# Setup divided into stages, constant products placed in TensorE's gaps, and all five queues reordered, in a four-layer graph network on one core

## What is computed

```
x = layernorm(x + L0(x, adj))     # multi-head attention, 4 heads of 32, scores masked by adj
x = layernorm(x + L1(x, adj))     # graph attention: e = leaky_relu(s1[i] + s2[j]), masked softmax, @ h
x = layernorm(x + L2(x, adj))     # the same with 8 heads of 16, a log prior, output projection W_out
x = layernorm(x + L3(x, adj))     # relu(x@w1+b1); unmasked attention (256 wide) + elu + residual;
                                  # relu(@w2+b2); masked attention (128 wide) + elu + residual; relu
```

## Time and profile before

| | |
|---|---|
| median of 3 runs | 1126.12 us (1124.22 to 1127.83) |
| profiled execution, its own time | 1126.89 us |
| its span, first to last instruction | 1125.1 us |
| TensorE busy | 997.7 us (89%) |
| VectorE busy | 917.5 us (82%) |
| ScalarE busy | 734.3 us (65%) |
| GpSimd busy | 397.1 us (35%) |
| mean granted TensorE clock | 0.970 |

### The profile page before, as it was taken

One profiled execution on the slowest core, in us unless ns is written; L12 is line 12 of the kernel. 1 busy time (PEld: TensorE's weight loads), 2 busy tenths in 40 slices (PEclk: granted clock), 3 DMA queues, 4 the chain that ended last, 5 costly groups with the idle time before them and its releaser, 6 DMA issues.

```text
span 1125.1 us, 26002 instructions
## 1 busy us (share of the span) xinstructions
PE 997.7 (89%) x8821; PEld 727.6 (65%) x8821; DVE 917.5 (82%) x2530; ACT 734.3 (65%) x1901; POOL 397.1 (35%) x781
## 2 busy tenths in 40 slices
PE   2899888999999999999999999999999998778673
PEld 1566655858677776767676776767676867455452
DVE  4467979988899898989889998989898988876432
ACT  1698756766768686877768685867777674432522
POOL 0113233323443342625243433426252334341421
PEclk9999989999999999999999999999999999988976
DMA  4001111102020202011020202020020202010000
GB/s 121 1 11 59 39 58 29 68 20 68 29 67 11 82 15 77 20 46 52 20 72 25 67 12 76 20 72 26 31 66 11 71 17 67 20 66 20 10 0 19
DMA packets 30994, 46.77 MB, mean 42 GB/s; under 512 B 7824, under 2 KB 10128, under 8 KB 30736
## 3 DMA queue, kind: packets, MB, share of 16 engines
q1 hardware_dynamic: 30864, 45.11, 12.8%
HBM read 40.64 MB, written 4.46 MB: 40 GB/s over the span
## 4 chain that ended last, share of the span: by engine, by line
PE 34%; DVE 25%; issue 8%; POOL 4%; ACT 3%; DVEq 0%; ACTq 0%; POOLq 0%
DVE P L1147 15%; PE bank L633 8%; PE bank L592 7%; PE bank L491 4%; PE bank L538 2%; POOL e L1308 2%; DVE stats_l L1006 2%; PE bank L470 2%; PE bank L499 2%; DVE l_P L1058 1%; ACT x L769 1%; PE bank L462 1%; DVE v L1178 1%; POOL rstd_l L1274 1%; DVE h_t L1183 1%
## 5 line engine op out<-in xcount | busy, mean ns | idle before, releaser
L1147 DVE SCALAR_TENSOR_TENSOR P<-row,t2e,mask_t 128x512 f32<-128x512 f32 x512 | 358.6, 760 | 18.3 <-DMA row<-line 15.3
L724 ACT ACTIVATE probs<-probs,neg_max 128x512 f32<-128x512 f32 x256 | 183.6, 718 | 13.1 <-DVE neg_max L970 13.0
L962 DVE CUSTOM_DVE_ANT_0 probs<-bank,mask_add 128x512 f32<-128x512 f32 x256 | 168.9, 676 | 13.0 <-PE bank L491 12.9
L734 ACT ACTIVATE probs_t<-bank 128x512 f32<-128x512 f32 x256 | 149.2, 601 | 10.8 <-PE bank L499 10.8
L499 PE MATMUL bank<-ident,probs 128*128 128x128 f32 x1024 | 137.4, 275 | 13.9 <-ACT probs L724 12.6
L769 ACT ACTIVATE x<-x,shift_l,rstd_l 128x128 f32<-128x128 f32 x256 | 105.3, 483 | 62.9 <-POOL shift_l L1281 62.8
L1308 POOL TENSOR_SCALAR e<-v 128x128 f32<-128x128 f32 x128 | 77.4, 632 | 171.2 <-ACT v L816 171.2
L499 PEld LDWEIGHTS bank<-ident,probs 128*128 128x128 f32 x1024 | 114.1, 141 | 28.9 <-ACT probs L724 24.5
L1266 POOL TENSOR_TENSOR rstd_l<-mv_l,ln_eps 128x4 f32<-128x4 f32 x64 | 19.3, 302 | 298.2 <-DVE mv_l L1016 298.1
L592 PE MATMUL bank<-P,GH 128*32 128x512 f32 x1024 | 117.4, 599 | 5.5 <-DVE P L1147 2.8
L633 PE MATMUL bank<-t,l_P 128*128 128x257 f32 x512 | 119.1, 383 | 1.1 <-DVE l_P L1072 1.1
(11 more groups left out here) (161 smaller groups left out, 1901.8 us busy)
## 6 DMA issues: line engine op xcount, KB each, us to landing
row<-line SPq DMA_DIRECT2D x128, 256.0 KB, 3.7
x_in<-in_x SPq DMA_DIRECT2D x16, 256.0 KB, 2.8
out<-x SPq DMA_DIRECT2D x16, 256.0 KB, 2.0
l_P<-in_adj SPq DMA_DIRECT2D x1, 1024.0 KB, 4.8
line<-turned SPq DMA_DIRECT2D x64, 4.0 KB, 1.5
w_fc<-in_L_gnn_W_fc SPq DMA_DIRECT2D x1, 256.0 KB, 3.4
probs_t<-in_L_gnn_a_fc SPq DMA_DIRECT2D x1, 256.0 KB, 6.1
w_cat<-in_L_gnn_W SPq DMA_DIRECT2D x2, 64.0 KB, 3.4
```

Source lines behind the costliest of these rows:

```text
L724: act.activation(e, e, ACT.Exp, bias=neg_max[:, m:m + 1], scale=SCALE0, accum_out=g.of(den0)[:, m:m + 1])\
L734: act.activation(probs_t[c % 2][:, h, :, :].rearrange("p j n -> p (j n)"), ps("l0_t", g, m)[:, :], ACT.Copy)\
L962: dve.tensor_tensor_reduce(probs[c % 2][:, h, :], ps("l0_s", g, m)[:, :], mask_add[:, c, :], 1.0, -3.0e38, ALU.add, ALU.max, row_max[:, m: ...
L1147: last = dve.scalar_tensor_tensor(P2[:, h % GROUP2, j, :], row(g, h)[:, :], g.of(t2e)[:, j, h:h + 1], mask_t[:, j, :], ALU.max, ALU.mult)
```

## The change

The setup becomes stages of the queues, with a semaphore each. On SP, nine loads (five weights and the four layer 0 biases) come first, on s_proj; then, as turns of SP's order, adj_load (the adjacency) and late_loads (fifteen loads for layers 1 to 3, on l1_in, l2_in, l3_in); then x. TensorE first makes twelve products of constants (WARM_UP) while it waits, transposes the five weights, waits for ScalarE's copies and starts its turns; the four mask blocks are the turns mask_T. VectorE's masks, folds and prior steps are turns (add_mask, one_mask, fold1, fold2, fold3, prior_in, prior_out). Its order begins: add_mask, one_mask, fold1, l0_v of graph 0, fold2, one l0_max, fold3, one l0_max, prior_in, two l0_max, l0_neg. The first user of each result waits for it, for graph 0 alone. The folds read their vectors from P2 instead of probs_t.

TensorE's order gets 102 turns "warm" (letter Z). Each makes two 128-column products of the identity and ones into the bank of the next stage, behind the wait for that bank and ahead of the stage's own waits; the stage then overwrites it. They stand in the new order as follows: one each before l0_xT(1), l0_k(1) and l0_t(0); two before l0_t(3, 12), behind l2_y(0); and 97 from l0_t(15, 12) on, among them 6 before l3b_o of graph 14, 16 before l3_zT of graph 15, 3 before its l3b_s, 6 before its l3b_o and 13 before its l3_r, the last turn of TensorE.

The order strings of all five engines and the banks are new throughout. The work of the stages themselves is as before. In TensorE's new order, of graph 9 for instance, l0_q follows l0_xT by five transposes of exponentials, where it followed by some forty turns; l2_h and l3_m1 have likewise moved close behind l2_xT and l3_xT.

The diff, cut to its core:

```diff
+WARM_UP = 12
...
     "pe":
-        "a0c0b0d0a1e0e0c1b1d1f0f0f0f0e0f0g0f0f0f0e0f0f0g0f0f0e1f0f0g0f0f0e1f1g0h0f1f1i0f1e1f1f1f1g1f1e1j0a2f1"
...
+        "a0b0c0d00000e0e000Z0a1b1Z0c100d1Z0f0f0f0f0e0f0g0f0f0f0e0f0f0g0f0f0e1f0f0g0f0f0e1g0h0f1f1i0f1f1e1f1f1"
...
+        "Z0Z0Z0Z0Z0Z0DfDfZ0IeEfFfFfGfZ0Z0Z0HfZ0Z0Z0Z0Z0Z0JfJfZ0Z0Z0Z0Z0Z0Z0Z0Z0Z0Z0Z0Z0If",
...
     for name, g, k in turns("pe"):
+        if name == "warm":
+            continue
...
-            sp.dma_start(adj_i, adj.rearrange("(p c) n -> p c n", c=C)).then_inc(s_adj, 16)
...
+            def adj_load(g, k):
+                sp.dma_start(adj_i, adj.rearrange("(p c) n -> p c n", c=C)).then_inc(signal["adj_in"], 16)
+
+            def late_loads(g, k):
+                l1, l2, l3 = signal["l1_in"], signal["l2_in"], signal["l3_in"]
+                sp.dma_start(w1_cat[:, 2:2 + D], w["L1_gnn_W"]).then_inc(l1, 16)
...
             pe.wait_ge(s_const, 3)
-            pe.wait_ge(s_w, 16 * N_WEIGHT_DMAS)
+            for _ in range(WARM_UP):
+                pe.matmul(bank[BANKS - 1][:, 0:P], ident[:, :], ones[:, :], start=True, stop=True)
+            pe.wait_ge(s_proj, 16 * N_PROJECTION_DMAS)
...
-            pe.wait_ge(s_setup, 2)
+            pe.wait_ge(s_proj_t, 1)
+
+            def mask_T(g, j):
+                pe.wait_ge(*sig("one_mask", g, 1))
+                ps = empty("mask_T", g, j)
                 for c in range(C):
-                    last = pe.transpose(bank[0][:, c * P:(c + 1) * P], adj_m[:, c, j * P:(j + 1) * P], ident[:, :])
-                last.then_inc(s_pre_pe, 1)
+                    last = pe.transpose(ps[:, c * P:(c + 1) * P], adj_m[:, c, j * P:(j + 1) * P], ident[:, :])
+                last.then_inc(filled("mask_T", g, j), 1)
...
+            def keep_warm(stage, g, k):
+                ps = empty(stage, g, HEADS0 * k if stage == "l0_s" else k)
+                for c in range(2):
+                    pe.matmul(ps[:, c * P:(c + 1) * P], ident[:, :], ones[:, :], start=True, stop=True)
+
+            order = turns("pe")
+            for at, (name, g, k) in enumerate(order):
+                if name == "warm":
+                    keep_warm(*next(turn for turn in order[at:] if turn[0] != "warm"))
+                else:
+                    stages[name](g, k)
...
+            def fold3(g, k):
+                dve.wait_ge(*sig("l3_in", g, 9 * 16))
+                for q in range(2):
+                    fold_in(w3_fc[:, q, 0:1], w3_fc[:, q, 2:2 + HID], foldv[:, 512:768])
+                    fold_in(w3_fc[:, q, 1:2], w3_fc[:, q, 2:2 + HID], foldv[:, 768:1024])
+                fold_in(w3_hand[:, 0:1], w3_hand[:, 2:2 + D], foldv[:, 1024:1152])
+                fold_in(w3_hand[:, 1:2], w3_hand[:, 2:2 + D], foldv[:, 1152:1280])
+                dve.memset(folds[:, 2:3], 0.0).then_inc(signal["fold3"], 1)
```

More of the change, by code:

```diff
@@ L305, in build_program @@
         stored = [sem(f"stored{q}") for q in range(2)]
-        for name, n in [("x_biased", 1), ("neg_max0", 4), ("exp0", 16), ("den0_safe", 1), ("rden0_made", 1),
+        for name, n in [("adj_in", 16), ("l1_in", 2 * 16), ("l2_in", 4 * 16), ("l3_in", 9 * 16), ("add_mask", 1), ("one_mask", 1),
+                        ("fold1", 1), ("fold2", 1), ("fold3", 1), ("prior_in", 1), ("prior_exp", 1), ("prior_ln", 1),
+                        ("prior_out", 1), ("x_biased", 1), ("neg_max0", 4), ("exp0", 16), ("den0_safe", 1), ("rden0_made", 1),
                         ("l2_c4", 1), ("dmax8_diag", 1), ("small2_made", 2), ("exp2", 3), ("gh2", 1), ("rden2_made", 2), ("p2_made", HEADS2),
@@ L530, in l0_y, with project @@
                 last.then_inc(filled("l0_y", g), 1)
-            def project(stage, src, before, cat, width):
+            def project(stage, src, before, cat, width, folded):
                 def f(g, k):
@@ L612, in l3_m1 @@
                 pe.wait_ge(*took("l3_xT", g))
+                if g.i == 0:
+                    pe.wait_ge(*sig("l3_in", g, 9 * 16))
                 ps = empty("l3_m1", g, k)
@@ L621, in l3_h @@
                     pe.wait_ge(*took("l3_m1", g, 1))
+                if c == 0 and g.i == 0:
+                    pe.wait_ge(*sig("fold3", g, 1))
                 ps = empty("l3_h", g, c)
@@ L673, in _ @@
                 "l3_o": l3_o, "l3_zT": l3_zT, "l3_m2": l3_m2,
-                "l3_h2": project("l3_h2", out2_t, "l3_m2", w3_hand, D + 2), "l3b_dm": spread_max("l3b"),
+                "l3_h2": project("l3_h2", out2_t, "l3_m2", w3_hand, D + 2, "fold3"), "l3b_dm": spread_max("l3b"),
                 "l3b_s": spread_sources("l3b"), "l3_r": l3_r, "l3b_o": attend("l3b", t4),
             }
-            for name, g, k in turns("pe"):
-                stages[name](g, k)
+            def keep_warm(stage, g, k):
[8 more added lines that the diff above has]
+                    stages[name](g, k)
         @block.scalar
@@ L799, in l3_m1 @@
                 act.wait_ge(*wrote("l3_m1", g, k))
+                if g.i == 0:
+                    act.wait_ge(*sig("l3_in", g, 9 * 16))
                 if g.has(1):
@@ L954, in l0_max @@
                 dve.wait_ge(*wrote("l0_s", g, m))
+                if g.i == 0 and m == 0:
+                    dve.wait_ge(*sig("add_mask", g, 1))
                 if c < 2:
@@ L1141, in l2_p @@
                     dve.wait_ge(*sig("exp2", g, 3))
+                    if g.i == 0:
+                        dve.wait_ge(*sig("fold3", g, 1))
                     if g.has(1):
@@ L1214, in _ @@
             stages = {
+                "add_mask": add_mask, "one_mask": one_mask, "fold1": fold1, "fold2": fold2, "fold3": fold3,
+                "prior_in": prior_in, "prior_out": prior_out,
                 "l0_v": l0_v, "l0_max": l0_max, "l0_neg": l0_neg, "l0_den": l0_den, "l0_rcp": l0_rcp, "l0_o": l0_o,
```

378 lines of the change are left out of this document (194 added, 184 removed), and 8 rows, old and new, of the table STAGES.

## The result

| | before | after |
|---|---|---|
| median | 1126.6 us (4 runs, 1124.2 to 1127.8) | 1097.56 us (4 runs, 1097.38 to 1098.13) |
| span of the profiled execution | 1125.1 us | 1095.9 us |
| VectorE busy | 917.5 us | 925.4 us |
| mean granted TensorE clock | 0.970 | 0.985 |

The ratio of after to before is 0.9746, with an interval of 0.9729 to 0.9763: 29.0 us faster than the runs beside it, where 12.5 were forecast.

What follows compares the result with a forecast made beforehand. TensorE was taken to bound the middle, so other edits could win only at the two ends. From 1126.12 us, -3.5 (start) - 9.5 - 1 (clock) - 1 (order) + 2.5 (overrun) = -12.5 gave 1113.5 us, range 1099 to 1128.

Steps and rivals of the forecast that it cites:

- Part 1: Start: the staged setup lets graph 0 begin 9.7 us earlier, of which 3.5 us is kept.
- a sign of being wrong: Start: x landing later than 20 us, because the loads interfere, would show the forecast wrong.
- Part 2: Mainly the end: fillers hold TensorE's clock, winning 9.5 us there and 1 us earlier, and cost 2.5 us of overrun.
- an assumed 80%: End: share of the 12.2 us of clock gain expected to arrive, 9.5 us, as VectorE and GpSimd become late next.
- the overrun: Gaps of the last groups: fillers outlast the gap and delay the stage behind, 2.5 us together, bounds 0.9 and 8.
- Part 3: Middle: the new order has fewer tight links, 8 for 13, and slightly less idle time, -1 us.
- A: Rival, middle: TensorE stalls on ScalarE's copies of the transposed x, +19.5 us, net 1133; chance 13%.
- B: Rival, tail: filler overrun of 8 us and next-late engines take the clock's gain, 1120.6 us; chance 12%.
- C: Rival, whole kernel: full 9.7 us at the start, 12.2 of the clock, overrun only 0.9, 1103 us; chance 17%.
- D: Rival, half-clock stretches: each holds up the whole kernel by half its length, 28.5 us, giving 1094.6; chance 3%.
- E: Rival, tail: the clock falls all the same, fillers take 0.95 us a turn, net about 1140; chance 5%.

Runs made afterwards that it cites:

- e3: The kernel before with its old setup, given the new order strings and banks, without fillers: 1119.7 us (ratio 0.995).
- e1: The kernel after without the 102 warm turns and the twelve products ahead of the first wait: 1113.9 us (ratio 0.989).
- e11: The kernel before with the staged setup, its old order and 95 warm turns in the gaps of its tail: 1117.2 us (ratio 0.991).
- e2: The kernel before with the staged setup, its old order strings and banks, and no fillers: 1125.9 us (ratio 1.000).
- e4: The kernel before with TensorE's second l3b_o turn moved ahead of the fifth l0_t in ten graphs: 1126.8 us (ratio 1.000).
- e5: The kernel before with three of VectorE's masked-weight operations of layer 2 left out in graphs 1 to 15: 1118.8 us.
- e7: The kernel before with half of layer 0's TensorE products of the probabilities with v left out in graphs 1 to 15: 1123.8 us.

## Why the prediction was right and wrong

**Part 1, the start: right, by two errors that cancel.** The forecast had x sent for at 12.86 and landing 6.5 us later. It was sent for at 15.66, because three issues ahead of it took 1.34, 2.02 and 0.96 us, and landed 4.4 us later, at 20.07, just past the 20 us that the prediction named as a sign of being wrong. From there each step came within 1 us of its forecast, the fold included. At the last negated maximum of graph 0 the kernel after is 54.5 - 51.0 = 3.5 us ahead, the very number of the sum. But the term belongs to this order: e3 is 2.1 us behind before at that point and e1 3.8 us ahead, so in the new order the setup is worth 5.9, and in the old one 1.2 (none in e11, whose start is that of e2). Calling it a property of the setup was too simple, and that the number came out is luck.

**Part 2, the clock and the fillers: right for the old order, half of it for the new.** The terms were 9.5 + 1 - 2.5 = 8 us, worked out from rows of the kernel before with an assumed 80%. e11, the same order with fillers, gives 8.7 us. The new order has more of TensorE's work at the half level to give back (58.3 us against 36.3 in the old) and the fillers bring 16.3. The way of pricing, half of the work in those stretches and a part of that, held in both orders, with two thirds for the 80% that was assumed. The single entries: a turn took 0.457 us for 0.475; the overrun of the two largest groups is 0.3 and 0.5 us where 0.9 and 1.0 were forecast. From 999.70 us on the clock is 0.96, and not 1.00: 1029.9 to 1033.3 us and, behind TensorE's last work, 1091.3 us to the end are at the half level. What the early fillers brought can't be told: the half level is there from 162.9 to 169.7 us (in e1 from 140.1 to 143.5 and from 164.0 to 170.8), and graph 0's last add comes 1.1 us earlier than in e1, less than like kernels scatter. TensorE's busy time is 1028.9 us and not 1046: I added 48 us of fillers and forgot to take off the 14.8 us that I had just worked out for the work at the half level.

**Part 3, the order of the middle: here the prediction failed.** "I take -1 us" is the term that was mis-sized. The new order was ahead by 17.0 us at graph 11 (e3 against before), and is worth 19.6 us where the fillers keep its end from giving half of that back (e11 against after). With the other terms alone the forecast is 12.5 - 1 = 11.5 us, and e11, which has them alone, is 9.8 us faster than the kernel before. So the miss comes with this one step: 12.0 us of the order by itself for the 1 us, and 7.6 because it also leaves the fillers more to give back. Its reasoning failed twice. It counted short links between stages on TensorE's queue, 13 against 8, as if each cost the same; e4 shows that such a wait can be made shorter by more than half and the period stays. And it drew the bound at a third of the idle time, 10 us, without a reason. The row that was there to be used is TensorE's idle time itself: 18.4 us in nine periods, where the same stages in another order run with 5.9. Of the 14.1 us by which nine periods became shorter, 12.5 are idle time and 1.6 less busy time. From 200 to 950 us 1.8% of the time is idle, where the forecast said 4%.

The statement in the first part, "The middle is bound by TensorE", was half the truth for before. e5 and e7 show that VectorE was on the path there as much or more, 6.2 us against 2.3 for like cuts; the kernel after comes nearer to it, and even there only 8.2 of 15.2 us less work came back.

**The rivals.** A, a stalled middle: the wait for the normalised x, which shares its place with A's copies, did grow from 5.8 to 8.6 us, but ScalarE's copies of the transposed x made no wait over 1 us in sum. B, a tail gain eaten: e11 and after show that it was not. C, all goes well: its 9.7 us of the start did not come, 3.5 did. D's number, 1094.6, lies near the result by luck, and its mechanism is not what happened. There, each us at the half level counts a half. The fillers removed 76.5 us of it (91.3 to 14.8) for 16.3 us of time in the new order and 47.7 (64.0 to 16.3) for 8.7 in the old, 0.21 and 0.18 of a us each. The page "TensorE: Matmul & The Clock Gate" of the Trainium skill, under "Terms", gives the factor of a half; in this case that prices also the time in which TensorE does nothing, 33.0 of e1's 91.3 us. E, the clock falls all the same: no, 0.96 from 999.70 us on, and a turn takes 0.457 us, not 0.95. What was said against it is too strong, though: from 1029.9 to 1033.3 us TensorE is busy throughout, and the granted clock is 0.51.

## What to carry to other kernels

Where two engines are both over 80% busy in a repeating middle, take TensorE's whole idle time per period, times the periods, as the bound of what a new order may win (here two thirds of it came back), and test with less work on one engine and on both which of them the pace hangs on; short links between stages do not tell. Price products that hold the clock by half of TensorE's work in the stretches at the half level, two thirds of it here, and do so on the order that will be run: the new one had 58.3 us of work there and the old one 36.3, with the same idle time at the end. In the start, look at what the first input waits for on its queue: moving one load ahead of fifteen brought 6.8 us, more than the staging of the setup was forecast to.
